# VectorE's exponential block set ahead of maxima, score copies and FFN steps in every slot of a fused attention and expert layer

## The chip, the cores and the metric

The kernel runs on one core of a Trainium2 chip. The metric is the device time of one execution in microseconds (us), lower is better. Everything is computed in fp32. One core has TensorE (PE, matrix products), VectorE (DVE), ScalarE (ACT), GpSimd (POOL), and SyncE (SP), which here only starts transfers. Each engine works through its own list of instructions in order, and they meet through semaphores.

## The reference

One attention layer over 4 batches of 1024 rows of 128 values, with 16 heads of width 8, each head taken 16 times at 16 "wavelengths", and then a gated mixture of 8 small experts, each stage followed by a layer norm:

```python
def wl_step(acc, wl):                       # 16 wavelengths
    m = cpm[None, :, None, None]            # cos of a phase, per head
    scores = jnp.einsum('bhqd,bhkd->bhqk', Q * m, K * m) * SCALE
    scores = scores * jnp.cos(KERR * scores * scores)
    attn = jax.nn.softmax(scores, axis=-1)
    return (acc + jnp.einsum('bhqk,bhkd->bhqd', attn, V) * iw, None)
...
x = _layernorm(x + attention(x))
gates = top-2 of softmax(x @ router_w + router_b)
out = jnp.einsum('bte,ebtd->btd', gates[..., :E], gelu(x @ w1) @ w2) + gates[..., E:] * x
x = _layernorm(x + out)
```

So there are 64 (batch, head) pairs, and for each of them 16 exponentials of one and the same 1024 x 1024 score matrix at 16 scales.

## The kernel before

Where the product of the largest query and key values is small enough, as it is here, the cosine is 1 and the kernel takes its fast path. It treats the 64 heads n = 0 to 63 one after another, and for each head 16 **slots**, one for each wavelength `at` = 0 to 15. A slot is a piece of each engine's written-out list:

- **ScalarE** (`wavelength`, L593) writes exp(scale x scores) of a whole head, 128 x 8192, into one of two buffers of `ring`. In waves that VectorE shares (10 of 16 in heads 0 to 15, `EARLY_WAVES`; 9 of 16 in heads 16 to 63, `LATE_WAVES`) it leaves the last 1024 columns out. It may start wave w + 2 only when TensorE has finished weighing wave w (`slot_free`).
- **TensorE** (`head_products`) first weighs wave `at` (`weigh_values`, L705; L703 and L711 are VectorE's part, and the semaphore `slot_free` comes with the last of these). Then, in the same slot, it transposes finished sums (`transpose_numer`, L721), and makes the scores of head n + 1: in slots 0 to 3 two tiles each for the row maxima (`max_tile`, L653), in slot 4 `broadcast_rowmax` (L661), in slots 6 to 9 two shifted score tiles each (`shifted_tile`, L672). All of these go through the two halves of `sc`, so that a tile waits until VectorE has emptied the one two before it, and `broadcast_rowmax` until all eight maxima are there (`sc_free`).
- **VectorE** (`vector_head`) empties them: `reduce_max` (L823) in slots 0 to 3, `set_row` (L827) in slot 5, `copy_scores` (L833) in slots 6 to 9. Beside that it copies sums (`copy_numer`, L911, at the end of a group of two or three waves), normalises (L918 to L923), and makes its **exponential block**, the last 1024 columns of a shared wave, in two halves: `exponents` (L850 to L854, four instructions) and `polynomials` (L860 to L862, three). `early_blocks` and `late_blocks` say which half falls into which slot. Most slots have one half. Slots 11 and 14 have more: in an even late head slot 11 has `exponents` and `polynomials` of one block, and slot 14 both halves of the next head's first block. The block's intermediate values lie in `ring`, buffer 1, behind the columns that ScalarE leaves out.

From head 16 on, two heads at a time also carry one 128-row tile of the second stage (24 pairs of heads; the last 8 tiles come in a tail). The even head is `part` 1: in slots 5, 10, 11 and 13 VectorE does `tile_part_one_vector` (slot 10: sum and layer norm, the end of which releases TensorE's `tile_transpose` in slot 11, L738; slot 11: copy of the transposed tile to `tile_x1T`, L945; slot 13: router logits), and in slots 12 to 15 `copy_hidden` (L956). TensorE does `tile_slice` (L753) in slots 12 to 15 after weighing; slice 0 waits for `tile_x1T`. The odd head is `part` 2: ScalarE applies the gelu between its waves 3 and 4 (L632, with two table loads); TensorE has `tile_part_two` (L765) in slots 10 to 13 and VectorE `add_experts` in slots 12 and 13.

`vector_head` writes VectorE's order out by hand. In a slot it is: normalise, sums, `copy_numer`, then maxima, set row or score copies, then the tile's steps, and then the exponential block; `tile_gates` (slot 4) and `tile_finish` (slot 15) of part 2 follow.

Of the kernel before, what the change touches and what calls it, by code (L numbers as in the profile page):

```python
# [74 lines left out]
EARLY_WAVES = (1, 3, 5, 7, 9, 11, 12, 13, 14, 15)  # L75
# [12 lines left out]
def build(nc, x, wq, bq, wk, bk, wv, bv, wo, bo, pm, iw, rw, rb, w1, w2, out):  # L88
# [9 lines left out]
    with ctx:  # L98
# [736 lines left out]
        def exponents(dve, m, waves, block, odd, first=False):  # L835


            base, at = share(m, waves, block), stream(waves, block, odd)
            back = EARLY_BUFS if waves is EARLY_WAVES else LATE_BUFS
            score = scores[:, bass.ds(m % 2, 1), KT - 1, :].rearrange("p o s -> p (o s)")  # L840
            bits = vprobs[:, at, :].bitcast(I32)
            dve.wait_ge(sc_free, USES * (m + 1))
            if not first:
                dve.wait_ge(vexp_step, base)
                read = W * m + waves[block - back] if block >= back else W * (m - 1) + waves[block - back]
                dve.wait_ge(slot_free, SLOTS + read + 1)
            apart(dve)

            then = stepper(dve, vexp_step, base, [0])
            then(nc.vector.tensor_scalar(bits, score, scales_log2[:, bass.ds(waves[block] * H + m % H, 1)], LOWEST,  # L850
                                         ALU.mult, ALU.max))
            then(nc.vector.tensor_scalar(vpower[:, at, :].bitcast(I32), bits, EXPONENT, 0x40000000, ALU.bitwise_and, ALU.bitwise_xor))  # L852
            then(nc.vector.tensor_scalar(vmant.bitcast(I32), bits, MANTISSA, ONE, ALU.bitwise_and, ALU.bitwise_or))  # L853
            nc.vector.tensor_scalar(bits, bits, EXPONENT | MANTISSA, 0x40000000, ALU.bitwise_and, ALU.bitwise_xor).then_inc(vexp_step, 1)  # L854

        def polynomials(dve, m, waves, block, odd):
            base, probs = share(m, waves, block), vprobs[:, stream(waves, block, odd), :]
            dve.wait_ge(vexp_step, base + 4)
            then = stepper(dve, vexp_step, base, [4])
            then(nc.vector.scalar_tensor_tensor(probs, vmant, EXP2_GAMMA, probs, ALU.add, ALU.mult))  # L860
            then(nc.vector.scalar_tensor_tensor(vmant, vmant, EXP2_ALPHA, vmant, ALU.add, ALU.mult))  # L861
            nc.vector.scalar_tensor_tensor(probs, vmant, EXP2_BETA, probs, ALU.add, ALU.mult).then_inc(vexp_step, 1)  # L862

        def early_blocks(dve, n, at):
            waves, block = EARLY_WAVES, (at + 3) // 2
            if at < 11:
                step = exponents if at % 2 else polynomials
                step(dve, n, waves, block, 0)
            elif at == 11:
                exponents(dve, n, waves, 7, 0)  # L870
                polynomials(dve, n, waves, 7, 0)
            elif at == 12:
                exponents(dve, n, waves, 8, 0)
            elif at == 13:
                polynomials(dve, n, waves, 8, 0)
                exponents(dve, n, waves, 9, 0)
            elif at == 14:
                polynomials(dve, n, waves, 9, 0)
                exponents(dve, n + 1, waves, 0, 0)
            else:  # L880
                polynomials(dve, n + 1, waves, 0, 0)
                exponents(dve, n + 1, waves, 1, 0)

        def late_blocks(dve, n, at, odd, more):
            waves, block = LATE_WAVES, (at + 3) // 2
            if at < 10:
                step = exponents if at % 2 else polynomials
                step(dve, n, waves, block, odd)
            elif at == 10:
                polynomials(dve, n, waves, 6, odd)  # L890
                if odd:
                    exponents(dve, n, waves, 7, odd)
            elif at == 11:
                if not odd:
                    exponents(dve, n, waves, 7, odd)
                polynomials(dve, n, waves, 7, odd)
            elif at == 12:
                exponents(dve, n, waves, 8, odd)
            elif at == 13:
                polynomials(dve, n, waves, 8, odd)  # L900
            elif at == 14 and more:
                exponents(dve, n + 1, waves, 0, 1 - odd)
                polynomials(dve, n + 1, waves, 0, 1 - odd)
            elif at == 15 and more:
                exponents(dve, n + 1, waves, 1, 1 - odd)

        def copy_numer(dve, n, f):

            dve.wait_ge(slot_free, SLOTS + W * n + FILLS[f][-1] + 1)
            dve.wait_ge(tr_full, NF * n + f + START)  # L910
            nc.vector.tensor_copy(numer[:, :], pv[:, f % 2, :]).then_inc(pv_read, 1)  # L911

        def normalise(dve, n, g):

            js = len(FILLS[GROUPED[g][0]])
            dve.wait_ge(tr_full, NF * n + 2 * g + 2 + START)
            blocks = tr[:, 0, :].rearrange("p (m r) -> p m r", r=VC)[:, :, 0:js * VR].rearrange("p m (j c) -> p m j c", c=VR)
            nc.vector.reciprocal(recip[:, :, 0:js], blocks[:, :, :, D]).then_inc(norm_step, 1)  # L918
            dve.wait_ge(norm_step, NF * n + 2 * g + 1)
            nc.vector.tensor_tensor(coef[:, :, 0:js], recip[:, :, 0:js], wl_wide[:, g, :, :, 0:js].rearrange("p f t j -> p (f t) j"),  # L920
                                    ALU.mult).then_inc(norm_step, 1)
            dve.wait_ge(norm_step, NF * n + 2 * g + 2)
            nc.vector.tensor_tensor(parts[:, :, :, STACK * g:STACK * g + js].rearrange("p m d j -> p m j d"), blocks[:, :, :, 0:D],  # L923
                                    coef[:, :, 0:js].rearrange("p m (j o) -> p m j o", o=1).to_broadcast([P, 2 * KT, js, D]),
                                    ALU.mult).then_inc(tr_read, 1)

        def sum_wavelengths(dve, n):
            dve.wait_ge(tr_read, NF // 2 * (n + 1) + START)
            dve.wait_ge(att_stored, 32 * (n // H) + START)
            nc.vector.tensor_reduce(att[:, :, bass.ds((n % H) * D, D)], parts[:, :, :, :].rearrange("p (f t) d x -> p (t d) f x", f=2),  # L930
                                    axis=AX.XY, op=ALU.add).then_inc(att_made, 1)
# [47 lines left out]
        def vector_head(dve, n, i=None, part=0, then=None, more=True, carried=True, waves=LATE_WAVES):  # L979

            for at in range(W):
                if at == 1 and carried:
                    normalise(dve, n - 1, NF // 2 - 1)
                if at == 3 and carried:
                    sum_wavelengths(dve, n - 1)
                if at in (6, 12):
                    normalise(dve, n, at // 6 - 1)
                if at + 1 == W or FILL_OF[at] != FILL_OF[at + 1]:  # L990
                    copy_numer(dve, n, FILL_OF[at])
                if more:
                    if at < 4:
                        reduce_max(dve, n + 1, 2 * at)
                        reduce_max(dve, n + 1, 2 * at + 1)
                    elif at == 5:
                        set_row(dve, n + 1)
                    elif 6 <= at < 10:
                        if at == 6:
                            dve.wait_ge(probs_ready, W * n + START)  # L1000
                        copy_scores(dve, n + 1, 2 * (at - 6))
                        copy_scores(dve, n + 1, 2 * (at - 6) + 1)
                if at in TILE_SLOTS and part == 1:
                    tile_part_one_vector(dve, i, TILE_SLOTS.index(at), then)
                if at >= 12 and part == 1:
                    copy_hidden(dve, i, at - 12)
                if at in (12, 13) and part == 2:
                    add_experts(dve, i, at - 12, then)
                if waves is EARLY_WAVES:
                    early_blocks(dve, n, at)  # L1010
                else:
                    late_blocks(dve, n, at, part - 1, more)
                if at == 4 and part == 2:
                    tile_gates(dve, i, then)
                if at == 15 and part == 2:
                    tile_finish(dve, i, then)
# [541 lines left out]
```

## Time and profile before

| | us |
|---|---|
| median of 3 runs | 6975.69 (6973.81 to 6976.5) |
| profiled execution, its own time | 6975.18 |
| its span, first to last instruction | 6973.7 |
| ScalarE busy | 6796.0 (97%) |
| TensorE busy | 6097.9 (87%) |
| VectorE busy | 6061.4 (87%) |
| mean granted TensorE clock | 0.957 |

1.5 us of the execution lie outside the span. A row of a list in order of time gives the start and the duration in us, engine, line, operation, what it writes and reads, how many instructions are merged, and in brackets how long the engine stood idle before it and what released it. Waits of less than 0.15 us are not shown. The ends of TensorE's instructions are modelled.

### The profile page before, as it was taken

The page shows a single profiled execution, that of the slowest core. Times are in us where ns is not written, and L with a number is a line of the kernel's source. Part 1 is how long each engine was busy: PE and PEld are TensorE (multiplying, and loading weights), DVE is VectorE, ACT ScalarE, POOL GpSimd, SP SyncE. Part 2 cuts the span into 40 slices and gives each one's busy share as a digit, 9 for nine tenths or more (in the row PEclk, how much of TensorE's full clock was granted, in tenths as well). Part 3 has the DMA queues.
Part 4 walks back from the last instruction along what each step waited for, and adds up shares of the span by engine and source line. Part 5 has one row for each costly group of instructions (what it writes and reads, how often), then busy time and mean ns, then how long its engine had stood idle before and what let it go on. Part 6 is the DMA issues. An engine that isn't in the chain of part 4 may idle for free.

```text
span 6973.7 us, 125248 instructions
## 1 busy us (share of the span) xinstructions
PE 6097.9 (87%) x47364; PEld 2296.8 (33%) x47364; DVE 6061.4 (87%) x8039; ACT 6796.0 (97%) x1209; POOL 148.7 (2%) x244
## 2 busy tenths in 40 slices
PE   7888888888889888889888898888888888988888
PEld 3222222222333333333333333333333333333336
DVE  7998899899888888898888888888988888888884
ACT  6999999999999999999999999999999999999993
POOL 0000000000000000000000000000000000000000
PEclk8999999999999999999999999999999999999999
DMA  2000000000101001000010010010010100100100
GB/s 60 3 5 5 5 3 5 5 3 5 33 22 30 18 28 30 17 28 27 22 30 23 22 30 18 28 30 17 28 30 20 30 25 20 30 18 28 30 16 35
DMA packets 60481, 150.52 MB, mean 22 GB/s; under 512 B 11168, under 2 KB 27424, under 8 KB 59680
## 3 DMA queue, kind: packets, MB, share of 16 engines
q1 hardware_dynamic: 52960, 136.89, 6.3%
q0 software_dynamic: 2816, 3.68, 0.8%
q8 instruction: 414, 6.78, 0.4%
q10 hardware_dynamic: 4160, 2.10, 0.1%
q14 instruction: 131, 1.07, 0.0%
HBM read 132.14 MB, written 10.49 MB: 20 GB/s over the span
## 4 chain that ended last, share of the span: by engine, by line
ACT 48%; PE 35%; issue 13%; ACTq 4%; DVE 1%; DMA 0%; SPq 0%; DVEq 0%
ACT ring L593 46%; PE pv L705 23%; ACTq L590 3%; PE sc L753 3%; PE pv L711 3%; PE tr L721 2%; PE sc L765 2%; ACT tile_h L632 1%; PE sc L1337 1%; PE tr L1347 1%; PE sc L672 1%; PE sc L653 0%; ACT L632 0%; ACTq L591 0%; PE sc L290 0%
## 5 line engine op out<-in xcount | busy, mean ns | idle before, releaser
L593 ACT ACTIVATE ring<-scores 128x7168 f32<-128x7168 f32 (+1 forms) x1023 | 6581.5, 6529 | 7.3 <-PE pv L711 3.6
L705 PE MATMUL pv<-ring,vh 128*32 128x512 f32 x30400 | 3944.4, 627 | 821.8 <-ACT ring L593 812.8
L705 PEld LDWEIGHTS pv<-ring,vh 128*32 128x32 f32 x30400 | 992.8, 114 | 3422.5 <-issue 2081.5
L862 DVE SCALAR_TENSOR_TENSOR vprobs<-ring,vprobs 128x1024 f32<-128x1024 f32 x592 | 725.3, 1225 | 20.4
L861 DVE SCALAR_TENSOR_TENSOR ring<-ring 128x1024 f32<-128x1024 f32 x592 | 725.2, 1225 | 20.3
L860 DVE SCALAR_TENSOR_TENSOR vprobs<-ring,vprobs 128x1024 f32<-128x1024 f32 x592 | 721.2, 1218 | 7.1
L833 DVE COPY scores<-sc 128x1024 f32<-128x1024 f32 (+1 forms) x512 | 601.3, 1216 | 111.3 <-PE sc L672 111.3
L823 DVE TENSOR_REDUCE rowmax<-sc 128x1 f32<-128x1024 f32 x512 | 599.7, 1213 | 20.0 <-PE sc L653 12.8
L711 PE MATMUL pv<-vprobs,vlast 128*32 128x512 f32 x2368 | 613.0, 592 | 3.7 <-DVE vprobs L862 2.5
L703 PE MATMUL pv<-vpower,vlast 128*32 128x512 f32 x2368 | 613.7, 594 | 0.0
L850 DVE TENSOR_SCALAR vprobs<-scores,scales_log 128x1024 int32<-128x1024 f32 (+1 forms) x592 | 440.7, 744 | 43.9 <-DVE vprobs L862 25.2
L721 PEld LDWEIGHTS tr<-fold,numer 128*128 128x128 f32 x3072 | 371.6, 191 | 324.5 <-issue 322.9
L911 DVE COPY numer<-pv 128x512 f32<-128x512 f32 x384 | 263.5, 686 | 222.5 <-PE pv L711 193.0
L854 DVE TENSOR_SCALAR vprobs<-vprobs 128x1024 int32<-128x1024 int32 x592 | 415.1, 701 | 22.3 <-issue 2.1
L853 DVE TENSOR_SCALAR ring<-vprobs 128x1024 int32<-128x1024 int32 x592 | 411.4, 695 | 20.2
L852 DVE TENSOR_SCALAR vpower<-vprobs 128x1024 int32<-128x1024 int32 x592 | 411.1, 694 | 20.3
L721 PE MATMUL tr<-fold,numer 128*128 128x64 f32 x3072 | 424.3, 281 | 0.8 <-DVE numer L911 0.8
L653 PE MATMUL sc<-kt_,qt 8*128 8x512 f32 x2048 | 322.6, 645 | 0.6 <-DVE rowmax L823 0.4
L672 PE MATMUL sc<-qt,kt_ 9*128 9x512 f32 x2048 | 298.2, 645 | 3.1 <-DVE scores L833 1.7
L711 PEld LDWEIGHTS pv<-vprobs,vlast 128*32 128x32 f32 x2368 | 144.6, 110 | 368.7 <-issue 308.0
L765 PEld LDWEIGHTS sc<-tile_w,tile_h 128*128 128x128 f32 x1536 | 178.8, 192 | 60.4 <-issue 60.4
L765 PE MATMUL sc<-tile_w,tile_h 128*128 128x128 f32 x1536 | 195.8, 281 | 0.0
(161 smaller groups left out, 2572.9 us busy)
## 6 DMA issues: line engine op xcount, KB each, us to landing
tile_w<-in_L_ffn_w SPq DMA_DIRECT2D x192, 512.0 KB, 3.9
qt<-q_scratch SPq DMA_DIRECT2D x256, 36.0 KB
kt_<-k_scratch SPq DMA_DIRECT2D x256, 36.0 KB
ring<-in_L_ffn_w SPq DMA_DIRECT2D x2, 2048.0 KB, 10.5
ring<-in_L_attn_x ACTq DMA_DIRECT2D x4, 512.0 KB, 7.2
q_scratch<-ring SPq DMA_DIRECT2D x4, 512.0 KB, 3.9
k_scratch<-ring SPq DMA_DIRECT2D x4, 512.0 KB, 4.9
v_scratch<-ring SPq DMA_DIRECT2D x4, 512.0 KB, 5.0
```

Source lines behind the costliest of these rows:

```text
L593: nc.scalar.activation(ring[:, i % SLOTS, 0:cols], scores[:, bass.ds(n % 2, 1), :, :].rearrange("p o k s -> p (o k s)")[:, 0:cols], ACT.Ex ...
L703: nc.tensor.matmul(sums, vlast[:, buf, 0, window], vpower[:, at, cols], start=False, stop=final)
L705: last = nc.tensor.matmul(sums, vh[:, buf, kt, window], ring[:, w % SLOTS, kt * S + qh * HALF:kt * S + (qh + 1) * HALF], start=(first and ...
L711: last = nc.tensor.matmul(pv[g * VC:(g + 1) * VC, f % 2, :], vlast[:, buf, 1, window], vprobs[:, at, qh * HALF:(qh + 1) * HALF], start=Fal ...
L721: last = nc.tensor.matmul(tr[:, 0, at * 2 * VC:(at + 1) * 2 * VC], numer[:, blk * P:(blk + 1) * P], fold[:, :], start=True, stop=True)
L765: last = nc.tensor.matmul(sc[:, 1, e * P:(e + 1) * P], tile_h[:, col:col + P], tile_w[:, wi % 2, col - wi * WC:col - wi * WC + P], start=( ...
L823: nc.vector.tensor_reduce(rowmax[:, t:t + 1], sc[:, t % 2, :], axis=AX.X, op=ALU.max).then_inc(sc_free, 1)
L833: nc.vector.tensor_copy(scores[:, bass.ds(m % 2, 1), k, :].rearrange("p o s -> p (o s)"), sc[:, use % 2, :]).then_inc(sc_free, 1)
L850: then(nc.vector.tensor_scalar(bits, score, scales_log2[:, bass.ds(waves[block] * H + m % H, 1)], LOWEST, ALU.mult, ALU.max))
L860: then(nc.vector.scalar_tensor_tensor(probs, vmant, EXP2_GAMMA, probs, ALU.add, ALU.mult))
L861: then(nc.vector.scalar_tensor_tensor(vmant, vmant, EXP2_ALPHA, vmant, ALU.add, ALU.mult))
L862: nc.vector.scalar_tensor_tensor(probs, vmant, EXP2_BETA, probs, ALU.add, ALU.mult).then_inc(vexp_step, 1)
```

## The change

In every slot VectorE's exponential block is taken ahead of the maxima, set row, score copies, `tile_part_one_vector`, `copy_hidden` and `add_experts`. Normalise, sums and `copy_numer` stay ahead of it, and `tile_gates` and `tile_finish` behind. No instruction is added or removed, and no other engine's list changes.

```diff
@@ -989,6 +989,10 @@
                     normalise(dve, n, at // 6 - 1)
                 if at + 1 == W or FILL_OF[at] != FILL_OF[at + 1]:
                     copy_numer(dve, n, FILL_OF[at])
+                if waves is EARLY_WAVES:
+                    early_blocks(dve, n, at)
+                else:
+                    late_blocks(dve, n, at, part - 1, more)
                 if more:
                     if at < 4:
                         reduce_max(dve, n + 1, 2 * at)
@@ -1006,10 +1010,6 @@
                     copy_hidden(dve, i, at - 12)
                 if at in (12, 13) and part == 2:
                     add_experts(dve, i, at - 12, then)
-                if waves is EARLY_WAVES:
-                    early_blocks(dve, n, at)
-                else:
-                    late_blocks(dve, n, at, part - 1, more)
                 if at == 4 and part == 2:
                     tile_gates(dve, i, then)
                 if at == 15 and part == 2:
```

## Rows read from the trace of the kernel before

**Rows 1.** The page, busy time of each engine and its share of the span.

```profile
PE 6097.9 (87%) x47364; PEld 2296.8 (33%) x47364; DVE 6061.4 (87%) x8039; ACT 6796.0 (97%) x1209; POOL 148.7 (2%) x244
```

**Rows 2.** Waits of ScalarE, whole span: us in total, times, longest.

```profile
ACT ring L593 <- PE pv L711: 3.6, 9, 0.7
ACT ring L593 <- PE pv L705: 3.4, 7, 0.7
```

**Rows 3.** VectorE in order of time, head 8, slots 0 to 4.

```profile
908.30 2.35 DVE L823 TENSOR_REDUCE rowmax<-sc 128x1 f32<-128x1024 f32 x2
910.57 1.22 DVE L860 SCALAR_TENSOR_TENSOR vprobs<-ring,vprobs 128x1024 f32<-128x1024 f32 x1
...
928.03 2.35 DVE L823 TENSOR_REDUCE rowmax<-sc 128x1 f32<-128x1024 f32 x2
...
933.25 1.23 DVE L860 SCALAR_TENSOR_TENSOR vprobs<-ring,vprobs 128x1024 f32<-128x1024 f32 x1
```

**Rows 4.** TensorE in order of time, head 8, slot 4 to slot 6.

```profile
930.43 2.05 PE L661 MATMUL sc<-ident,rowmax 128*128 128x128 f32 x16 [0.15 <-DVE rowmax L823]
932.70 3.19 PE L705 MATMUL pv<-ring,vh 128*32 128x512 f32 x25 [0.22 <-ACT ring L593]
...
936.16 1.03 PE L711 MATMUL pv<-vprobs,vlast 128*32 128x512 f32 x4
939.63 3.64 PE L705 MATMUL pv<-ring,vh 128*32 128x512 f32 x32 [2.44 <-ACT ring L593]
```

**Rows 5.** VectorE in order of time, head 36, slots 6 to 11.

```profile
3891.90 0.46 DVE L918 RECIPROCAL recip<-tr 128x48 f32<-128x48 f32 x1 [0.61 <-PE tr L721]
...
3912.88 2.36 DVE L833 COPY scores<-sc 128x1024 f32<-128x1024 f32 x2 [1.94 <-PE sc L672]
...
3924.97 0.68 DVE L911 COPY numer<-pv 128x512 f32<-128x512 f32 x1
3925.57 0.28 DVE L945 COPY tile_x1T<-tr 128x128 f32<-128x128 f32 x1
...
3931.25 1.22 DVE L862 SCALAR_TENSOR_TENSOR vprobs<-ring,vprobs 128x1024 f32<-128x1024 f32 x1
```

**Rows 6.** TensorE in order of time, head 36, slot 11 to slot 15.

```profile
3923.66 0.33 PE L738 MATMUL tr<-ident,tile_x 128*128 128x128 f32 x1
3926.16 3.64 PE L705 MATMUL pv<-ring,vh 128*32 128x512 f32 x32 [2.17 <-ACT ring L593]
...
3930.67 2.00 PE L753 MATMUL sc<-tile_x1T,tile_w 128*128 128x128 f32 x16
...
3949.99 1.03 PE L711 MATMUL pv<-vprobs,vlast 128*32 128x512 f32 x4
```

**Rows 7.** TensorE in order of time, head 30, slot 12.

```profile
3285.79 5.34 PE L705 MATMUL pv<-ring,vh 128*32 128x512 f32 x32 [2.17 <-ACT ring L593]
...
3292.00 2.00 PE L753 MATMUL sc<-tile_x1T,tile_w 128*128 128x128 f32 x16
```

**Rows 8.** ScalarE in order of time, head 30 wave 15 to head 31 wave 1.

```profile
3298.53 6.19 ACT L593 ACTIVATE ring<-scores 128x7168 f32<-128x7168 f32 x1 [0.65 <-PE pv L711]
3305.16 7.03 ACT L593 ACTIVATE ring<-scores 128x8192 f32<-128x8192 f32 x1 [0.44 <-PE pv L711]
3312.46 19.18 ACT L593 ACTIVATE ring<-scores 128x7168 f32<-128x7168 f32 x3 [0.27 <-PE pv L711]
```

**Rows 9.** TensorE's slow weighings: head 28 slot 6, head 18 slot 8, head 20 slot 11.

```profile
3034.20 5.34 PE L705 MATMUL pv<-ring,vh 128*32 128x512 f32 x32 [2.18 <-ACT ring L593]
...
1983.07 5.34 PE L705 MATMUL pv<-ring,vh 128*32 128x512 f32 x32 [1.37 <-ACT ring L593]
...
2215.30 4.89 PE L705 MATMUL pv<-ring,vh 128*32 128x512 f32 x25 [2.40 <-ACT ring L593]
```

**Rows 10.** Window of head 18's weighing 8: us, busy times, then PEclk, DMA share, GB/s.

```profile
1982.91:1988.50 5.59, 5.43 (x36) 1.43 (x40) 4.35 (x7) 5.59 (x2) 0.00 (x0) 0.69 0.02 4
```

**Rows 11.** Groups by line: ScalarE's gelu.

```profile
L632 ACT ACTIVATE tile_h<-tile_h 128x4096 f32<-128x4096 f32 x24 | 86.8, 3618 | 0.3
```

## The prediction, made before the changed kernel was run

> **What bounds the kernel now.** I read the busy times first. ScalarE is busy 97% of the span, TensorE and VectorE 87% each [rows 1]. The second look is at ScalarE's waits: in all of its 1023 long exponentials it waited 7.0 us for TensorE [rows 2]. So ScalarE is the bound, and between its first and last exponential it has nothing to win back. Anything that holds up TensorE's weighing long enough to stop it costs the full amount. The third look is at what TensorE has in hand. It begins most weighings after standing idle for 2.2 to 2.4 us, released by ScalarE [rows 4, 6], and ScalarE needs wave w weighed only when it has finished wave w + 1. VectorE hands TensorE three things: emptied halves of `sc`, copied sums, and exponential blocks. The change makes the last earlier and the first later, so I follow the first.
>
> **The change part by part.** The same instructions run on VectorE. Where VectorE never idles, a slot ends when it did before, only its contents are swapped: what stood ahead of the block is late by the block, 2.9 us for `exponents` (930.38 to 933.25 in [rows 3]) and 3.7 us for `polynomials` (910.57 to about 914.2, from there on the same three instructions each time, 1.22 us and a gap of 0.03).
>
> *Early heads, slots 0 to 4.* From 908.30 to 933.25 VectorE works without a pause [rows 3]. The last pair of maxima, ended at 930.38, now ends where the slot ends, at 933.2. `broadcast_rowmax` waits for it; before, it started at 930.43 [rows 4]. It then runs 933.3 to 935.3 (2.05 us), and weighing 5 behind it takes 937.19 - 932.70 = 4.49 us [rows 4]: it ends at about 939.8. ScalarE wants it when its wave 6 ends, which is when TensorE takes up wave 6, 939.6 (exponential 7 starts about 0.1 before). With 0.1 us for the handover ScalarE starts at 939.9 instead of 939.5: **0.4 us lost**, in each of heads 1 to 15, 6.2 us. In slots 0 to 3 the maxima are late by a block too, 2.9 or 3.7 us, and hold up the score tiles and the weighing behind them. But part of that falls into the pause of about 2.4 us that TensorE has anyway [rows 4], a weighing may end that much later again before ScalarE misses it, and the delays do not add up, since each slot starts anew from ScalarE's end. Only in slot 4 does the long broadcast stand between the last maximum and the weighing. In slots 6 to 9 the block fills VectorE's own idle time ahead of the score copies, and the copies end later by less than the 3.7 us of a block, which the same two margins cover. Slots 12 to 15 of an early head hold nothing that is moved.
>
> *Late heads, part 1, slots 11 and 12.* Here the largest block, both halves, passes one small copy. In head 36 `tile_x1T` is copied at 3925.57 to 3925.85, and the block ends at 3932.47 [rows 5]. Slice 0 starts at 3930.67, straight behind the transposes [rows 6], so the copy now comes when TensorE already waits for it. How late, call it d, depends on when VectorE gets to slot 11. VectorE's work from the normalising in slot 6 to the end of slot 11 is 3932.47 - 3891.90 = 40.57 us, of which 1.94 were idle, waiting for the last score tiles [rows 5]. With the block ahead of the copies that idle time is used, which leaves 38.6 us. But `copy_numer` in slot 11 waits for weighing 11 (ended when L738 starts, 3923.66 to 3923.73 [rows 6]), and from it to the end of slot 11 are 3932.47 - 3924.97 = 7.50 us [rows 5]. So the copy ends at 3923.8 + 7.5 = 3931.3: d = 0.6.
>
> What does d cost? From slice 0 on, TensorE runs without a pause to the end of weighing 15 at 3951.02 [rows 6]. The trace holds the experiment. In head 30 weighing 12 took 5.34 us instead of 3.64 [rows 6, 7] and slice 0 began 1.7 us late; ScalarE then stood 0.65, 0.44 and 0.27 us [rows 8], where it normally overlaps by 0.1 each time, together 1.7. So **d is lost in full**, once for each pair.
>
> d is larger where a weighing ran slow. The clock granted in such a window was 0.69 of full speed [rows 10], that is 1.2 GHz for about half of it and 2.4 GHz for the rest, after a pause of 1.4 to 2.4 us [rows 9]; the weighing is 1.7 us longer. Of the 24 pairs, 5 have it in slot 6 (the first of them is head 28), 6 in slot 8 (head 18) and 7 in slot 11 (head 20) [rows 9], 4 in none of these, 2 in slot 12 (heads 30 and 56 [rows 7]). Slot 6 slow: VectorE starts its 38.6 us 1.7 us later, and d = 38.6 - (3930.67 - 3891.90 - 1.7) = 1.5. Slot 8 slow: its `copy_numer` waits 1.2 us more, less what slot 11 absorbs, d = 1.1. Slot 11 slow: 0.6 + 1.7 = 2.3. Slot 12 slow: slice 0 is late anyway, d = 0. The sum is 5 x 1.5 + 6 x 1.1 + 7 x 2.3 + 4 x 0.6 = **32.6 us**.
>
> *The rest, at nothing, with its cover.* `tile_x1` comes 3.7 us later in slot 10, less what idle time gives back; TensorE's L738 then runs at most until weighing 12, which ScalarE releases after 2.17 us of idle time [rows 6]. Without that cover it would add to d. `copy_hidden` in slots 12 to 14 is passed by up to 6.6 us, but slice k + 2 needs copy k only two slots later. The last of them, in slot 15, is wanted by the next head's maxima behind weighing 0, and by the gelu after wave 3, three slots on. Slots 0 to 3 of part 2 lie ahead of the gelu and its table loads [rows 11], during which TensorE catches up. In slots 12 and 13 `add_experts` is passed by the block, which fills a wait for `tile_part_two`; that makes VectorE early at the next head, whose broadcast so keeps a margin that the early heads don't have. SyncE's loads of weights and heads wait for TensorE's tiles, and they move with d. GpSimd's list is not passed. One wait moves ahead: in early odd slots `exponents` waits for the weighing of that same slot, and maxima or copies now queue behind it. Their tiles come behind that weighing too, so nothing waits longer. The tail has none of these slots.
>
> Sum: 6975.2 (the profiled execution) + 6.2 + 32.6 = 7014.0. The median of the runs was 0.5 us above that execution, so **7014** stands for the median too, 0.55% slower.
>
> **The rivals.**
>
> *The clock falls elsewhere.* The new waits are pauses of TensorE: 2.1 us ahead of `broadcast_rowmax` in early heads, d ahead of slice 0. Pauses of 1.4 to 2.4 us stood ahead of the slow stretches [rows 9], yet most pauses of that size had none behind them. If the slow 1.7 us came to all 15 broadcasts and to slot 11 in all pairs, the cost would be 15 x 2.1 + 24 x 2.3 = 87 us: 7062. Against it: slots 6 and 8 lose their pauses, since later score tiles fill them, and slow stretches there may vanish. If they vanished everywhere, d would be 0.6 in all 24 pairs and the time 6975.2 + 14.4 + 6.2 = 6996. The Trainium skill (TensorE: Matmul & The Clock Gate, "What's actually happening") says that the slow clock is the default and that activity releases it. By that rule pauses that are filled help and new ones hurt, which is both of these cases; the trace agrees that the slow stretches follow pauses.
>
> *Not slower: the delay is absorbed.* Before slot 12 VectorE wins back idle time, as the 1.94 us [rows 5]. If it came to the copy of `tile_x1T` within about 0.2 us of the transposes' end, the pairs would cost nothing, and only a gain was left: ScalarE's 7.0 us of waits [rows 2] is all there is, so 6968 at best, up to 6982 with the early heads' 6.2. It decides from d = 0, and the end of weighing 11 plus 7.5 us forbids that, unless the part behind `copy_numer` runs quicker. The Trainium skill (Perfetto Trace Analysis, "Optimization Strategy") says to look for the gaps on the most contended engine and let their dependencies start sooner. The only gaps on ScalarE are those 7.0 us, and none of them comes from VectorE's block.
>
> *It does nothing*, because VectorE waits at the block for the same weighing as before. For the early odd slots that is so, but not for the other slots, where the block's operands are ready.
>
> **How the numbers follow.** The forecast, 7000 to 7030, has 0.60. The clock falling on the new pauses, above 7030, has 0.20. No slow stretches, about 6990 to 7000, has 0.08. Absorbed or without effect has 0.12. The range 6988 to 7060 takes in the first, the third, and most of the second, and leaves out two in ten. About 0.2%, 14 us, is what a measurement can tell from no change: slower 0.88, within it 0.10, faster 0.02.
>
> **What would show it.** Right: ScalarE's waits for L711 and L705 rise from 7 to some 40 us, with pieces of 0.6 to 2.3 us in slots 14 to 16 of the even late heads and 0.4 us at wave 7 of the early ones. TensorE waits for `tile_x1T` ahead of L753 and longer for L823 ahead of L661. VectorE's waits for L672, L653 and L753 shrink. Wrong: L753 still starts straight behind the transposes; or ScalarE stands elsewhere, such as waves 3 to 5 or 9 to 11, which would mean that the maxima or score copies went past the margin; or the mean clock falls below 0.95.

## The result, and the profile after

The change made the kernel slower by nearly three times what was forecast.

| | us |
|---|---|
| before, median | 6974.75 |
| after, median of 4 | 7084.51 (7080.73 to 7087.77) |
| ratio | 1.0157, 95% interval 1.0144 to 1.017 |
| profiled execution of after, span | 7086.3 |
| mean granted TensorE clock | 0.952 (0.957 before) |

The direction was right, the size was not: 110 us against 39, and outside the range, whose upper end was 7060.

The page of after, busy times, to set beside [rows 1]:

```profile
PE 6276.2 (89%) x47364; PEld 2364.2 (33%) x47364; DVE 6053.4 (85%) x8039; ACT 6808.4 (96%) x1209; POOL 191.2 (3%) x244
```

The work is the same, the counts are too. TensorE is "busy" for 178 us more although no product was added: the same ones run more slowly, or tile by tile with a wait between where they overlapped. ScalarE's waits of after (us in total, times, longest), to set beside [rows 2]:

```profile
ACT ring L593 <- PE pv L711: 54.7, 88, 3.2
ACT ring L593 <- PE pv L705: 52.0, 19, 3.8
```

7.0 us have become 106.7, so the waits make 99.7 of the 112.6 us by which the span grew. Most of the rest is the overlap of 0.1 us that each of the 107 waits takes away (an estimate: 10.7 us). What TensorE waited for in after:

```profile
PE sc L653 <- DVE rowmax L823: 48.1, 20, 3.0
PE sc L753 <- DVE tile_x1T L945: 37.7, 22, 2.5
PE sc L661 <- DVE rowmax L823: 35.5, 28, 1.5
PE sc L672 <- DVE scores L833: 34.7, 68, 1.3
```

Two of these were forecast, L753 behind `tile_x1T` and L661 behind the maxima. The longest sum was not: `max_tile` (L653) with pieces of up to 3.0 us. Neither were the waits ahead of the score tiles (L672), which are short.

**Where the time went.** I took the distance from each head's first exponential to the next head's. In early heads it was 102.2 us before, and it is 105.7 to 105.9 in after from head 2 on. Against 15 times 102.2, heads 1 to 15 lose 51 us (1 in the trace of before). A pair of late heads took 212.6, and 23 pairs lose 61 (8 in the trace of before). Head 0 adds 4 and the last pair 5. Nearly all of the loss stands at two places.

*Early heads, slots 1 to 3.* TensorE in order of time, head 8 of after:

```profile
931.96 3.19 PE L705 MATMUL pv<-ring,vh 128*32 128x512 f32 x25 [0.32 <-ACT ring L593]
...
935.42 1.03 PE L711 MATMUL pv<-vprobs,vlast 128*32 128x512 f32 x4
939.34 3.21 PE L653 MATMUL sc<-kt_,qt 8*128 8x512 f32 x8 [2.89 <-DVE rowmax L823]
942.48 5.21 PE L705 MATMUL pv<-ring,vh 128*32 128x512 f32 x32
947.61 1.14 PE L653 MATMUL sc<-kt_,qt 8*128 8x512 f32 x8
```

Weighing 1 ends at 936.45. The next score tiles need the half of `sc` that slot 0's maxima read, and VectorE makes these only behind its polynomials:

```profile
936.92 1.22 DVE L862 SCALAR_TENSOR_TENSOR vprobs<-ring,vprobs 128x1024 f32<-128x1024 f32 x1
938.07 2.35 DVE L823 TENSOR_REDUCE rowmax<-sc 128x1 f32<-128x1024 f32 x2
```

So TensorE pauses 2.89 us. What comes behind the pause is slow: the tiles take 3.21 us instead of 1.14 (1.1 us of it is the wait for the second maximum), the weighing 5.21 instead of 3.64. Windows of after over the pause, the tiles and the weighing (columns: us, busy x5, granted clock, DMA share, GB/s):

```profile
936.50:939.30 2.80, 0.00 (x0) 0.00 (x0) 2.77 (x4) 2.80 (x2) 0.00 (x0) 0.92 0.00 0
939.30:942.50 3.20, 3.16 (x12) 1.03 (x12) 3.10 (x6) 3.20 (x1) 0.00 (x0) 0.50 0.00 0
942.50:945.90 3.40, 3.40 (x22) 0.88 (x24) 3.33 (x5) 2.40 (x1) 0.00 (x0) 0.53 0.00 0
```

The granted clock is 0.50, the lower level of 1.2 GHz, from the end of the pause on. Weighing 2 ends at 947.7, and ScalarE, whose wave 3 ended at 944.9, stands until then:

```profile
918.80 26.10 ACT L593 ACTIVATE ring<-scores 128x8192 f32 x4
947.95 20.03 ACT L593 ACTIVATE ring<-scores 128x8192 f32 x3 [3.05 <-PE pv L705]
```

*Late heads, slot 12.* Slice 0 waits for `tile_x1T` as forecast. In order of time, TensorE in heads 36 and 38 of after, to set beside the row of L753 in [rows 6]:

```profile
4011.40 3.40 PE L753 MATMUL sc<-tile_x1T,tile_w 128*128 128x128 f32 x16 [2.31 <-DVE tile_x1T L945]
...
4226.93 2.05 PE L753 MATMUL sc<-tile_x1T,tile_w 128*128 128x128 f32 x16 [1.32 <-DVE tile_x1T L945]
```

Head 38 is the usual case: 14 of the 24 pairs stand at about 1.3 us and lose 1.6. Eight more stand like head 36. Their weighing 11 was slow; they stand 2.3 us, and then the slices themselves take 3.40 us instead of 2.0, at the lower clock. These lose 3.9 each. The last pair pauses 1.4 us and has slow slices too, and loses 3.2. The first has a slow weighing 12 instead and loses 1.7. Together that is 58 us. From the slices to wave 1 of the odd head nothing is made up, as [rows 8] had shown.

### The profile page after: what moved, and what is told of

It is laid out like the page before. It is cut to its first block, busy times and chain, and to the rows that moved or that the text cites. A ratio compares the mean times of both kernels' runs of the same rounds, so it can differ in the third digit from the quotient of the medians.

```text
span 7086.3 us, 125226 instructions
## 1 busy us (share of the span) xinstructions
PE 6276.2 (89%) x47364; PEld 2364.2 (33%) x47364; DVE 6053.4 (85%) x8039; ACT 6808.4 (96%) x1209; POOL 191.2 (3%) x244
## 4 chain that ended last, share of the span: by engine, by line
ACT 36%; PE 32%; DVE 14%; issue 14%; ACTq 3%; DVEq 0%; DMA 0%; SPq 0%
ACT ring L593 35%; PE pv L705 20%; PE sc L753 3%; DVE ring L861 3%; DVE vprobs L860 3%; ACTq L590 3%; PE pv L711 2%; PE sc L765 1%; DVE vprobs L850 1%; PE tr L721 1%; DVE ring L853 1%; DVE vpower L852 1%; PE sc L653 1%; ACT tile_h L632 1%; DVE scores L833 1%
## 5 line engine op out<-in xcount | busy, mean ns | idle before, releaser
L653 PE MATMUL sc<-kt_,qt 8*128 8x512 f32 x2048 | 385.5, 676 | 48.3 <-DVE rowmax L823 48.1
L672 PE MATMUL sc<-qt,kt_ 9*128 9x512 f32 x2048 | 394.5, 646 | 36.8 <-DVE scores L833 34.7
L753 PE MATMUL sc<-tile_x1T,tile_w 128*128 128x128 f32 x1536 | 207.8, 292 | 39.1 <-DVE tile_x1T L945 37.7
L753 PEld LDWEIGHTS sc<-tile_x1T,tile_w 128*128 128x128 f32 x1536 | 191.6, 203 | 62.2 <-issue 42.9
```

The lines of the kernel that those rows point to most:

```text
L753: last = nc.tensor.matmul(sc[:, k % 2, j * P:(j + 1) * P], tile_w[:, k % 2, j * P:(j + 1) * P], tile_x1T[:, :], start=True, stop=True)
```

## The experiments

Each ran beside the kernel before, whose median was 6973.2 to 6974.4 in them. The four groups below ask: which heads, which slot, which cause, and what is left.

**Which heads: the early and the late ones by themselves.**

```diff
+                ahead = waves is EARLY_WAVES          # a_early_only
+                ahead = waves is LATE_WAVES           # b_late_only
+                if ahead: block()                     # ahead of the maxima ...
...
+                if not ahead: block()                 # where it stood before
```

Here and below `block()` stands for the call of `early_blocks` or `late_blocks`; the comments are mine, and the diffs are shortened.

> The block is taken ahead in heads 0 to 15 only; heads 16 to 63 keep the old order. From the two traces the early heads became 3.6 us longer each (pitch of ScalarE's wave 0 from 102.2 to 105.8), so if the two groups of heads don't act on each other this costs about 53 us: 7028. My prediction on record had 6 us here (6981). The rival, that most of the loss sits in the 48 late heads, gives under 7000.

Measured: 7027.15, ratio 1.0076 (1.006 to 1.0093).

> The other half: the block is taken ahead in heads 16 to 63 only. From the traces: even late heads 1.2 us longer (two in three) or 3.5 us (one in three), odd ones 0.4, together 57 us: 7032. The prediction on record had 33 us here (7008). If the two halves add up, a_early_only and this one together make the 110 us of the change; if the order in early heads disturbs the late ones, the sum falls short.

Measured: 7027.97, ratio 1.0079 (1.0062 to 1.0095). The two losses, 54.0 and 54.8 us, add up to 108.8, against 109.8 for both together. The forecast had 6 and 33. So there are two losses that don't act on each other, as far as totals can tell that are uncertain by some 11 us each. Both were undersized, the early one by nearly nine times.

**Which slot: one slot of each by itself.**

```diff
+                ahead = waves is EARLY_WAVES and at == 0                    # i_slot0_only
+                ahead = part == 1 and at == 11 and waves is LATE_WAVES      # j_slot11_only
```

> Of the early heads' order only slot 0 is changed: the polynomials go ahead of the first two maxima, everything else stands as before. Theory A (one slot does it: the first two maxima come 3.7 us later, TensorE pauses up to 2.9 us in slot 1 and then works at the low clock, and ScalarE misses the weighing of wave 2): most of the early loss, 40 to 50 us, 7015 to 7025. Theory B (the lateness has to pile up over slots 0 to 4 until broadcast_rowmax): under 10 us, at most 6985.

Measured: 7022.02, ratio 1.0072 (1.0055 to 1.0089). 48.8 of the 54 us come from one slot, with the polynomials ahead of two maxima.

> Of the late heads' order only slot 11 of the even heads is changed: both halves of the block go ahead of the copy of tile_x1T. Theory A (this one copy is the late loss): VectorE ends slot 11 1.8 to 2.4 us after TensorE wants slice 0, and does not win back the idle time of slots 6 to 10 as in the full change, so 2.1 us x 24 = 50 us, and up to 1.4 us more each where TensorE's pause brings the low clock: 7025 to 7060. Theory B (the late loss comes from score copies and hidden copies): under 10 us.

Measured: 7026.0, ratio 1.0077 (1.006 to 1.0094). One copy of 0.28 us, passed by 6.6 us of block, makes 52.8 us, as much as all of the late heads' new order. VectorE does not win back idle time here, so the wait is longer than in after (1.9 to 2.2 us in nearly all pairs), but the slices ran slow in only four of the 24. In total TensorE waited for `tile_x1T`:

```profile
PE sc L753 <- DVE tile_x1T L945: 46.4, 23, 2.3
```

**Undoing the same slots.** Here the theory of the one slot fell. In e_both_undone the copy is also left out at its old place.

```diff
+                ahead = not (waves is EARLY_WAVES and at == 0)              # d_slot0_undone, e_both_undone
+                if at == 11 and part == 1:                                  # e_both_undone, ahead of the block
+                    tile_part_one_vector(dve, i, 2, then)
```

> The full change, but in slot 0 of the early heads the two maxima stand ahead of the polynomials again. Theory A (slot 0 is the cause): 40 to 49 us come back, 7035 to 7045. Theory B (slots 1 to 4 would do the same without slot 0, since their maxima are as late): the low clock moves to slot 2 or 3 and less than 20 us come back, above 7065.

Measured: 7075.54, ratio 1.0146 (1.0129 to 1.0163). Only 9 us came back. The low clock had moved to the first slot that still has late maxima. TensorE in head 8, slots 2 and 3, and ScalarE there:

```profile
940.14 3.21 PE L653 MATMUL sc<-kt_,qt 8*128 8x512 f32 x8 [2.96 <-DVE rowmax L823]
943.28 4.95 PE L705 MATMUL pv<-ring,vh 128*32 128x512 f32 x25
```

```profile
949.64 6.18 ACT L593 ACTIVATE ring<-scores 128x7168 f32 x1 [3.18 <-PE pv L711]
```

It is the same pause, the same slow tiles, the same 3 us, one slot later. Slot 0 was enough for the loss but not needed for it.

> The full change, but slot 0 of the early heads and the copy of tile_x1T in slot 11 of the even late heads stand ahead of the block. Everything else (17 kinds of slot) keeps the new order. Theory A (the two places are the whole loss): within 10 us of the kernel before, 6975 to 6985. Theory B (the other maxima, score copies, tile_x1 and hidden copies cost too): over 6990.

Measured: 7030.81, ratio 1.0078 (1.0062 to 1.0095). Against d_slot0_undone the copy of `tile_x1T` in its old place gives 44.7 us back, and no pair's slices wait for it in the trace. What is left, 57 us, is nearly all in the early heads (51 by the distances of their first exponentials).

> As e_both_undone, but in the early heads the maxima of slots 0 to 3 all stand ahead of the block, so that TensorE finds no late maximum in slots 1 to 4. What remains changed is set row, the score copies, the FFN steps except the tile_x1T copy, and the maxima of the late heads. Theory (late maxima bring a 3 us pause of TensorE in whichever slot has the first late pair, and the low clock with it): the 44 to 57 us that e_both_undone still loses go, 6975 to 6985. Rival (another moved step of the early heads, set row or the copies, loses them): above 7010.

```diff
-                ahead = not (waves is EARLY_WAVES and at == 0)
+                ahead = not (waves is EARLY_WAVES and at < 4)
```

Measured: 6981.68, ratio 1.0013 (1.0003 to 1.0022). With the early maxima and the one copy in their old places 103 of the 110 us are gone. The new order of set row, score copies, `tile_x1`, logits, hidden copies, expert sums and the late heads' maxima together costs about 7 us (2 to 15 by the interval). In its trace ScalarE's two waits above 1 us are 2.76 us at wave 4 of head 16, behind a pause of 2.89 us ahead of the tiles of slot 1 as in the early heads, and 1.39 at wave 10 of head 5. In the later even heads the first of these tiles doesn't wait.

**Which cause: lateness, or the clock behind the pause.** The same late VectorE, with TensorE kept at work in the pause. The four products are read by nobody.

```diff
                 weigh_values(pe, n, buf, at, waves)
+                if at == 1 and waves is EARLY_WAVES:
+                    for _ in range(4):
+                        nc.tensor.matmul(tr[:, 1, :], ident[:, :], head_q[:, 0:HALF], start=True, stop=True)
```

> i_slot0_only (7022, slot 0 of the early heads alone) with the four unread products of f_busy_slot1 between weighing 1 and the next score tiles, which fill TensorE's pause of 2.9 us and delay nothing. Clock theory: ScalarE's loss of 3.05 us a head goes almost in full, 6974 to 6985. Rival (VectorE's lateness by 3.7 us costs by itself): at least half of the 49 us stays, above 6997.

Measured: 6981.39, ratio 1.0011 (1.0002 to 1.0021), where i_slot0_only had 7022.02: 41 us are back. Against the kernel before beside each, 7 us are left of 49, and in heads 1 to 15 ScalarE waits 0.5 us in the trace, where it waited 40.8. The first maximum of head 8 ends 2.1 us behind weighing 1; in i_slot0_only it is 2.8. TensorE in the same stretch, i_slot0_only first, then m_slot0_only_busy (head 8 each; L778 are the four products):

```profile
930.20 3.21 PE L653 MATMUL sc<-kt_,qt 8*128 8x512 f32 x8 [2.87 <-DVE rowmax L823]
933.34 5.20 PE L705 MATMUL pv<-ring,vh 128*32 128x512 f32 x32
```

```profile
912.44 3.70 PE L778 MATMUL tr<-qt,ident 128*128 128x512 f32 x8
916.07 1.14 PE L653 MATMUL sc<-kt_,qt 8*128 8x512 f32 x8
917.14 3.64 PE L705 MATMUL pv<-ring,vh 128*32 128x512 f32 x32
```

And the window of m_slot0_only_busy over those tiles and the weighing:

```profile
916.00:920.80 4.80, 4.80 (x45) 1.34 (x44) 4.34 (x6) 4.80 (x1) 0.00 (x0) 1.00 0.00 0
```

The products took 3.70 us, not the 2.5 that I had expected, so the tiles start 3.6 us behind weighing 1, 0.7 later than in i_slot0_only. Yet the granted clock is 1.00, and ScalarE waits 9.4 us in the whole kernel. A TensorE that does useless work through the pause is faster here than one that waits. The earlier maximum doesn't explain it, since the tiles start later all the same; it does spare them the wait between the two maxima.

> The full change, and in slot 1 of the early heads TensorE has four products of its own that nobody reads (identity by 512 columns of the query rows, into a part of PSUM that early heads don't use; about 2.5 us) between weighing 1 and the next score tiles. They fill the pause of 2.9 us there and delay nothing. Clock theory (of the 3.1 us that ScalarE loses at wave 4, some 2.5 are tiles and a weighing at the low clock behind that pause): granted clock back to 1.0 there, 30 to 38 us back, 7047 to 7055. Rival (the loss is VectorE's lateness alone, the clock comes along): 7084, or more.

Measured: 7050.65, ratio 1.0109 (1.0092 to 1.0126): 34 us back from the full change, of the 54 that the early heads lose there. The rest is of two kinds: ScalarE now waits 1.2 to 1.5 us in 9 of heads 1 to 15. Four of these waits are at wave 4. There weighing 0 ran slow and weighing 1 ended 1.3 us late, and the products themselves then hold the tiles up. Five are at wave 5, behind a weighing 3 that took 6.2 us instead of 4.5.

> The full change, and in slot 12 of the even late heads TensorE has eight products of 128 columns that nobody reads (about 1.0 us) between its transposes and the wait for tile_x1T. Clock theory: only the 8 pairs in which the slices ran at the low clock behind a pause of 2.3 us (1.4 us each) gain, at most 11 us: 7073. Rival (the clock has no part in the late loss): 7084. If the products delay slice 0 the time rises.

```diff
             if k == 0:
-                pe.wait_ge(tile_x1T_made, i + 1)
                 pe.wait_ge(sc_free, USES * (m + 1))
+                for _ in range(8):
+                    nc.tensor.matmul(sc[:, 0, 0:P], ident[:, :], wo_sb[:, :], start=True, stop=True)
+                pe.wait_ge(tile_x1T_made, i + 1)
```

Measured: 7085.16, ratio 1.0158 (1.0141 to 1.0175), no difference from after. By itself this total would say that the clock has no part in the late loss, but the trace says otherwise. The slices run at 2.0 us in all 24 pairs, and a pair with a slow weighing 11 loses 2.3 us where it lost 3.9. But such pairs have become 18 instead of 8, and that eats most of the gain: the losses at slot 12 come to 53 us in this trace, where after had 58. The products also took 2.0 us, twice what I had meant. They hold up five of the other six pairs by 0.2, and the first pair by 1.8. This run settles the slices' 1.4 us and nothing about the total.

**What is left: the size of the step, and the score copies.**

> The kernel before, but in slot 11 of the even late heads only the first half of the block (exponents, 2.9 us) goes ahead of the copy of tile_x1T, and the polynomials stay behind. In the trace of before the copy ends 4.5 us ahead of slice 0, so by the deadline theory 2.9 us are free: 6970 to 6980. A theory by which each us of lateness costs in proportion (6.6 us cost 2.2 us a pair) gives 2.9/6.6 of j_slot11_only's 53 us: 6997.

```diff
+                if at == 11 and part == 1:
+                    exponents(dve, n, waves, 7, 0)      # moved here from late_blocks, slot 11
                 if at in TILE_SLOTS and part == 1:
                     tile_part_one_vector(dve, i, TILE_SLOTS.index(at), then)
```

Measured: 6974.2, ratio 1.0001 (0.9991 to 1.001). The same copy passed by 2.9 us instead of 6.6 costs nothing. The cost is not in proportion; it begins at a deadline. In before the copy ends 4.2 to 4.8 us ahead of slice 0 in 21 of the 24 pairs, and 6.6 less 4.5 is 2.1, near the 2.2 us a pair that j_slot11_only lost.

> The kernel before, with the block ahead of the score copies only (slots 6 to 9, all heads). As I read the traces the block fills VectorE's own wait for score tiles and the copies stay inside TensorE's margin: no difference, 6970 to 6980. If late copies bring pauses and the low clock as the maxima do, over 6990.

```diff
+                ahead = 6 <= at < 10
```

Measured: 6981.59, ratio 1.0012 (1.0003 to 1.0022). This is small but not nothing: 7 us for the order that I had counted free. It is of the size of what k_maxima_undone keeps, and k_maxima_undone has this step in it. The trace of h_copies_only shows where it arises. ScalarE stands at wave 10 in six heads (0, 1, 34, 44, 58 and 62), 1.4 to 3.4 us each and 12.1 together, where it never stood in before (this execution took 6985.95, 4 us more than the median). Head 34 in slots 7 and 8, TensorE and then ScalarE:

```profile
3688.95 3.16 PE L672 MATMUL sc<-qt,kt_ 9*128 9x512 f32 x8 [0.92 <-DVE scores L833]
3692.04 6.08 PE L705 MATMUL pv<-ring,vh 128*32 128x512 f32 x32
```

```profile
3698.26 7.04 ACT L593 ACTIVATE ring<-scores 128x8192 f32<-128x8192 f32 x1 [3.10 <-PE pv L705]
```

It is the loss of the early heads once more: a tile waits for VectorE, here only 0.92 us, and the tiles (3.16 us, part of it a wait between the two) and the weighing (6.08 instead of 3.64) behind it run at the low clock: 0.70 granted over the tiles and 0.50 from 3692.05 to 3695.40. Of 68 such waits in this trace, six are followed by a loss.

## Why the prediction was wrong, point by point

**What bounds the kernel: right.** ScalarE had nothing to gain, and its 7 us of waits became 107.

**The late copy in slot 11: the mechanism right, the size off.** The term that was mis-sized is "The sum is 5 x 1.5 + 6 x 1.1 + 7 x 2.3 + 4 x 0.6 = 32.6 us"; the pairs lose 58 there in the trace of after (3 in that of before). Three things were missing in d. First, its last link, the handover from the end of the copy to slice 0: 0.24 us in 22 of the 24 pairs, 5 us. The 7.5 us from `copy_numer` to the end of the copy were right (7.51 measured), but I had let slice 0 start with that end. Second, behind the pause that d makes the clock is sometimes low, and the slices then take 1.4 us more, in nine pairs: 12 us. Where it falls is not the pause's length alone: in j_slot11_only 20 of 24 pairs paused 1.9 to 2.2 us ahead of slices at full speed. Third, the slow weighings were counted at the places where they had stood. They moved: slot 8 has them in 15 of the even heads instead of 8, slot 6 in none, slot 11 in 8. With my own values of d that is worth only 2 us, and the first pair's slow weighing 12 another 2. With the handover, 2.3 + 0.24 + 1.4 is the 3.9 us of the pairs with a slow weighing 11. The usual pair comes to 1.1 + 0.24 = 1.3 of its 1.6: VectorE reached slot 11 some 0.2 us later than I had it. That d is lost in full held.

**The early heads: the step that failed** is "In slots 0 to 3 the maxima are late by a block too ... But part of that falls into the pause of about 2.4 us that TensorE has anyway [rows 4], a weighing may end that much later again before ScalarE misses it". I looked only at how late the tiles would come. That by itself nearly fits into the margin: with the pause filled, m_slot0_only_busy loses 7 us where i_slot0_only loses 49. But the pause brings the lower clock for the tiles and the weighing behind it. In head 8 of after these take 3.21 and 5.21 us; at a clock of 1.00 they take 2.26 and 3.64 (head 2 of i_slot0_only, below), 2.5 us less. ScalarE stands 3.05 there, so by this estimate the clock is five sixths of it and the lateness 0.5 us. The two together do not fit. The forecast put the early loss into slot 4, 0.4 us a head (15 of these are 6.0, not the 6.2 of the sum). In after the excess is 3.6 us a head, 3.05 of it a wait at wave 4, and at wave 7 ScalarE waits in one head only, 0.56 us. That is head 1, which loses nothing at wave 4, so the mechanism of slot 4 is there, and the larger loss before it hides it. The prediction had named this sign of being wrong itself: ScalarE standing at "waves 3 to 5 or 9 to 11, which would mean that the maxima or score copies went past the margin". The mean clock stayed just above its bound of 0.95, at 0.952.

I also walked through head 8 of before only, and that head is of a kind that shortens the pause. Its weighing 0 ran slow, so that weighing 1 ended 1.3 us late, shortly before a late maximum would. The trace of i_slot0_only has heads of both kinds in one run. Head 2, whose weighing 0 ran slow, and the tiles behind its weighing 1:

```profile
291.38 4.90 PE L705 MATMUL pv<-ring,vh 128*32 128x512 f32 x28 [2.13 <-ACT ring L593]
...
304.08 2.26 PE L653 MATMUL sc<-kt_,qt 8*128 8x512 f32 x8 [0.84 <-DVE rowmax L823]
306.26 3.64 PE L705 MATMUL pv<-ring,vh 128*32 128x512 f32 x32
```

The window over them, in the same trace:

```profile
304.08:309.90 5.82, 5.82 (x44) 1.60 (x44) 5.68 (x9) 5.82 (x2) 0.00 (x0) 1.00 0.00 0
```

With the same order on VectorE the pause is 0.84 us, the clock stays at 1.00, and heads 2 and 3 lose nothing. Heads 7 to 15 pause about 2.9 us and lose 3.5 to 3.6 each, all of them. But the short pause is no safe one. Heads 4, 5 and 6 have the same slow weighing 0 and the same pause, and lose 3.2, 3.3 and 2.0. Head 4 of the same trace, TensorE and then windows:

```profile
508.56 3.08 PE L653 MATMUL sc<-kt_,qt 8*128 8x512 f32 x8 [0.84 <-DVE rowmax L823]
511.57 6.16 PE L705 MATMUL pv<-ring,vh 128*32 128x512 f32 x32
```

```profile
508.56:511.60 3.04, 3.04 (x12) 0.71 (x13) 2.97 (x5) 3.04 (x2) 0.00 (x0) 0.71 0.00 0
511.60:514.60 3.00, 3.00 (x18) 0.76 (x20) 2.93 (x5) 3.00 (x1) 0.00 (x0) 0.50 0.00 0
```

So a slow weighing 0 saved two heads of five. What decides between them I have not settled.

**The rival of the clock** was the right one, and it had 0.20 and the wrong place. It was priced at the two pauses that the sum already knew (ahead of `broadcast_rowmax`, ahead of slice 0), 7062. The pause that mattered, ahead of the tiles in slot 1, was not on the list, because the part before had called it covered. By the rule that I drew from the Trainium skill (TensorE: Matmul & The Clock Gate, "What's actually happening": the slow clock is the default and activity releases it) it should have been; the trace of after agrees with the rule, with 0.50 granted behind the pause. The two cases of the rival both came in part. Where the early heads' pause was filled, slow weighings became fewer: 17 in heads 1 to 15 of m_slot0_only_busy against 43 in i_slot0_only, 28 in f_busy_slot1 against 45 in after. Where slot 12's was filled they only moved: 45 in the even late heads of g_busy_slot12 against 48. One reading was a little off: a mean of 0.69 between the levels 0.5 and 1.0 means the low one for about six tenths of the window, not half.

**What cost nothing did so,** nearly. `tile_x1` in slot 10, the logits, the hidden copies and `add_experts` were given as covered; k_maxima_undone has them all moved and loses 7 us, with the score copies among them. The score copies I had at nothing, and they measure 7, by the same step that failed in the early heads: a wait that fits the margin, with a low clock behind it that does not.

**Not slower, and does nothing:** both fell, with the ratio's interval from 1.0144 up.

## What to carry to other kernels

When work is pushed back on a helper engine, price two things at each consumer: how late it becomes, and what its pause does to it. In these runs a pause of TensorE of 0.8 to 2.9 us was followed, often but not always, by 1.4 to some 3 us of extra time at the low clock, and margins that cover the wait need not cover both. A reordered step is free up to a deadline and then costs in full, if no such pause comes with it, so look at the largest block passing the smallest hand-over first: here 6.6 us passed a copy of 0.28 us and cost 53 us, while 2.9 us passed it for nothing. And before a slot is called covered, walk through more than one kind of repetition in the trace, since the one looked at may be the one in which a slow stretch elsewhere shortens the pause.

## What the runs showed of the hardware that was not expected

- The granted clock fell to 0.50 behind pauses of TensorE of 2.9 us (head 8 of after), of 2.3 us (ahead of the slices of head 36), and of only 0.84 us (head 4 of i_slot0_only) and 0.92 us (head 34 of h_copies_only). Length alone does not decide: it stayed at 1.00 behind the same 0.84 us in head 2 of i_slot0_only, one pause of 1.4 us in after had slow slices behind it, and 20 of 1.9 to 2.2 us in j_slot11_only had not. What does decide is open.
- Filling the pause with useless products kept the clock at 1.00 and made the kernel 41 us faster than the same order with the pause.
- Slow stretches can move when one is taken away. With slot 0's maxima back in place, slots 2 and 3 had them; with slot 12's pause filled, weighing 11 was slow in 18 pairs instead of 8. With slot 1's pause filled, they did become fewer. The early heads settled at 105.8 us in after and in d_slot0_undone alike, though the loss stood in different slots. Why both settle at the same length I have not settled.
- Four fp32 products of 128 x 512 took 3.70 us in that slot, and eight of 128 x 128 took 2.0 us, each as two matrix instructions.
